# Decoder block on one core: the shift by the maxima in the mixing stage, half of it moved from TensorE to VectorE

## The reference, cut to what matters

```
logits = (x @ phi_w.T + phi_b)            # tokens x (64 experts x 32 slots)
C = softmax(logits, axis=2)               # over the 64 experts, for each token and slot
Y = einsum('tznp,npH->tzH', C, Y_tilde)   # mix 2048 slot outputs into each token
x = layernorm(x + Y)
```

## Time and profile before

| | us |
|---|---|
| median of 3 runs | 1799.91 (1797.38 to 1803.08) |
| the profiled execution's own time | 1800.99 |
| its span, first to last instruction | 1799.2 |
| PE busy in the span | 1625.1 (90%) |
| DVE busy | 1269.0 (71%) |
| POOL busy | 897.9 (50%) |
| ACT busy | 805.4 (45%) |
| first `mix_L` matmul starts at | 1215.82 |
| last `mix_res` starts at | 1796.54 |

### The profile page before, as it was taken

How to read it: one execution, slowest core, us unless ns; L and a number is a source line. 1 busy time by engine, 2 the same in 40 slices (tenths; PEclk the granted TensorE clock), 3 DMA queues, 4 the chain that set the end, 5 groups by cost and what they waited for, 6 DMA issues and landing times. The chain is left out here.

```text
span 1799.2 us, 43419 instructions
## 1 busy us (share of the span) xinstructions
PE 1625.1 (90%) x16382; PEld 1321.2 (73%) x16382; DVE 1269.0 (71%) x2438; ACT 805.4 (45%) x1354; POOL 897.9 (50%) x848
## 2 busy tenths in 40 slices
PE   6776698988988989699999999979999999999998
PEld 5665476766766767477777777758999999999997
DVE  5998366666655666688888888866666666766665
ACT  2444143333333334355665566544444444444443
POOL 3333222222222222299999999954555555555554
PEclk8787599889988889899999999999999999999999
DMA  4110100000000000300000000000000000000000
GB/s 136 30 30 7 30 7 7 7 6 7 7 6 7 7 6 4 95 1 0 0 0 0 0 0 0 0 1 4 7 10 7 10 7 10 7 10 8 8 10 9
DMA packets 20165, 22.79 MB, mean 13 GB/s; under 512 B 2013, under 2 KB 14366, under 8 KB 20002
## 3 DMA queue, kind: packets, MB, share of 16 engines
q1 hardware_dynamic: 18402, 15.95, 3.2%
q0 software_dynamic: 1088, 4.19, 0.8%
q10 hardware_dynamic: 512, 0.23, 0.0%
HBM read 16.18 MB, written 4.19 MB: 11 GB/s over the span
## 5 line engine op out<-in xcount | busy, mean ns | idle before, releaser
L1295 POOL TENSOR_TENSOR mix_c<-mix_e,mix_rinv 128x1024 f32<-128x1024 f32 x128 | 243.5, 1902 | 135.7 <-DVE mix_rinv L1281 133.2
L1261 DVE TENSOR_REDUCE mix_mx<-mix_L 128x16 fp32r<-128x1024 f32 x128 | 156.8, 1225 | 166.7 <-PE mix_L L1217 166.7
L1016 POOL TENSOR_TENSOR gather_d<-gather_e,gather_rinv 128x1024 f32<-128x1024 f32 x128 | 245.0, 1914 | 50.8 <-DVE gather_rinv L991 42.8
L1232 PEld LDWEIGHTS mix_Y<-kept_phi,mix_cT 128*128 128x128 f32 x2048 | 248.2, 192 | 10.5 <-ACT mix_cT L1248 3.7
L1232 PE MATMUL mix_Y<-kept_phi,mix_cT 128*128 128x128 f32 x2048 | 249.5, 275 | 2.9 <-ACT mix_cT L1248 2.9
L1248 ACT COPY mix_cT<-mix_T 128x1024 f32<-128x1024 f32 x128 | 130.1, 1016 | 210.8 <-PE mix_T L1239 210.8
L782 POOL TENSOR_TENSOR cross_veps<-cross_mv,kept_eps 128x1 f32<-128x1 f32 x64 | 12.2, 190 | 383.2 <-DVE cross_mv L729 383.2
L959 ACT ACTIVATE gather_e<-gather_L 128x1024 f32<-128x1024 f32 x128 | 131.3, 1025 | 155.4 <-PE gather_L L926 155.4
L981 DVE TENSOR_REDUCE gather_mx<-gather_L 128x32 fp32r<-128x1024 f32 x128 | 156.8, 1225 | 34.5 <-PE gather_L L907 28.7
L987 DVE TENSOR_REDUCE gather_rsum<-gather_e 128x32 f32<-128x1024 f32 x128 | 156.2, 1220 | 32.0 <-ACT gather_e L959 30.5
L1252 ACT ACTIVATE mix_e<-mix_L 128x1024 f32<-128x1024 f32 x128 | 131.1, 1024 | 105.2 <-PE mix_L L1222 105.2
(11 more groups left out here) (201 smaller groups left out, 3722.6 us busy)
## 6 DMA issues: line engine op xcount, KB each, us to landing
attn_xTg<-in_xT SPq DMA_DIRECT2D x16, 256.0 KB, 2.6
kept_xres<-in_x POOLq DMA_DIRECT2D x4, 1024.0 KB, 11.4
out<-mix_res SPq DMA_DIRECT2D x32, 128.0 KB, 1.8
cross_cg<-in_ctxT SPq DMA_DIRECT2D x32, 58.5 KB, 1.7
setup_wT<-in_w_qkvT SPq DMA_DIRECT2D x1, 192.0 KB
kept_consts<-in_consts SPq DMA_DIRECT2D x1, 68.0 KB
first_xq<-in_xq ACTq DMA_DIRECT2D x1, 64.0 KB, 2.7
setup_wproj<-in_w_proj SPq DMA_DIRECT2D x1, 64.0 KB
```

The lines of the kernel that those rows point to most:

```text
L1016: pool.tensor_tensor(dd[tu.par][ju][:].rearrange("p i (n s) -> p i n s", n=16), e[ju][:], rinv[ju][:].rearrange("p (i n) -> p i n", i=2).u ...
L1232: ins = pe.matmul(psY[t % 2][:, 0:128], cT[u % 2][:, c, :], w.yk[:, 8 * (u % 2) + c, :], start=(u % 2 == 0 and c == 0), stop=(u % 2 == 1 a ...
L1261: dve.tensor_reduce(mx[u % 2][:].rearrange("t (i p) -> t i p", i=2), psL[u % 2][:].rearrange("t i (p n) -> t i p n", p=8), X, ALU.max)\
L1295: pool.tensor_tensor(cc[u % 2][:], e[u % 2][:], rinv[u % 2][:].unsqueeze(2).to_broadcast([128, 16, EXPERTS]), ALU.mult)\
```

## The change

- DVE gets a new instruction in each unit, behind the maxima: it subtracts the maxima of slots 0 to 7 from bank 0 and writes the result to a new SBUF tile `mix_low` (128 x 512, two buffers). It waits for its own maxima (`mx_ready`) and for the exponential that last read the buffer, and signals `low_ready`.
- PE shifts only bank 1: one matmul of 512 columns in place of two. Before it overwrites a pair of banks it waits for `low_ready` of unit u-2 too.
- ACT takes the exponential in two halves of 512: bank 1 from PSUM once the shift is done, then `mix_low` from SBUF once `low_ready` has come. `e_ready` is signalled by the second.

```diff
--- before.py
+++ after.py
@@ -1165,6 +1165,7 @@
     with ExitStack() as ctx:
         st = Store(nc, ctx, "mix")
         mx = [st.sb(f"mx{i}", [128, 16], F32R) for i in range(2)]
+        low = [st.sb(f"low{i}", [128, 8, EXPERTS]) for i in range(2)]
         e = [st.sb(f"e{i}", [128, 16, EXPERTS]) for i in range(2)]
         sums = [st.sb(f"sums{i}", [128, 16]) for i in range(2)]
         rinv = [st.sb(f"rinv{i}", [128, 16]) for i in range(2)]
@@ -1180,8 +1181,8 @@
         psT = st.ps("T", [128, 8, 128])
         psY = [st.ps(f"Y{i}", [128, 512]) for i in range(2)]
 
-        (l_made, mx_ready, shifted, e_ready, sum_done, rinv_ready, c_ready, cT_made, cT_ready, cT_read) = (
-            st.sem(n) for n in ("l_made", "mx_ready", "shifted", "e_ready", "sum_done", "rinv_ready", "c_ready",
+        (l_made, mx_ready, low_ready, shifted, e_ready, sum_done, rinv_ready, c_ready, cT_made, cT_ready, cT_read) = (
+            st.sem(n) for n in ("l_made", "mx_ready", "low_ready", "shifted", "e_ready", "sum_done", "rinv_ready", "c_ready",
                                 "cT_made", "cT_ready", "cT_read"))
         y_done, st_done, mv_ready, ve_done, rstd_ready, res_ready = (
             st.sem(n) for n in ("y_done", "st_done", "mv_ready", "ve_done", "rstd_ready", "res_ready"))
@@ -1211,6 +1212,7 @@
                 for u in units(k, 0):
                     at = slice(u // 2 * 128, u // 2 * 128 + 128)
                     reach(pe, e_ready, u - 1)
+                    reach(pe, low_ready, u - 1)
                     for n, (xs, ws) in enumerate(((w.xh, w.w2h), (w.xl, w.w2h), (w.xh, w.w2l))):
                         for i in range(2):
                             c = (2 * (u % 2) + i) * 512
@@ -1218,11 +1220,9 @@
                     ins.then_inc(l_made, 1)
                 for u in units(k, 1):
                     pe.wait_ge(mx_ready, u + 1)
-                    for i in range(2):
-                        ins = pe.matmul(psL[u % 2][:, i, :], w.neg_ident[:],
-                                        mx[u % 2][:, 8 * i:8 * i + 8].unsqueeze(2).to_broadcast([128, 8, EXPERTS]),
-                                        start=False, stop=True, skip_group_check=True)
-                    ins.then_inc(shifted, 1)
+                    pe.matmul(psL[u % 2][:, 1, :], w.neg_ident[:],
+                              mx[u % 2][:, 8:16].unsqueeze(2).to_broadcast([128, 8, EXPERTS]),
+                              start=False, stop=True, skip_group_check=True).then_inc(shifted, 1)
                 for u in units(k, 3):
                     t = u // 2
                     pe.wait_ge(cT_ready, u + 1)
@@ -1249,8 +1249,9 @@
                 for u in units(k, 1):
                     act.wait_ge(shifted, u + 1)
                     reach(act, c_ready, u - 1)
-                    act.activation(e[u % 2][:].rearrange("t p n -> t (p n)"),
-                                   psL[u % 2][:].rearrange("t i x -> t (i x)"), ACT.Exp).then_inc(e_ready, 1)
+                    act.activation(e[u % 2][:, 8:16, :], psL[u % 2][:, 1, :].rearrange("t (p n) -> t p n", p=8), ACT.Exp)
+                    act.wait_ge(low_ready, u + 1)
+                    act.activation(e[u % 2][:, 0:8, :], low[u % 2][:], ACT.Exp).then_inc(e_ready, 1)
 
         @block.vector
         def _(dve):
@@ -1261,6 +1262,11 @@
                     dve.tensor_reduce(mx[u % 2][:].rearrange("t (i p) -> t i p", i=2),
                                       psL[u % 2][:].rearrange("t i (p n) -> t i p n", p=8), X, ALU.max)\
                         .then_inc(mx_ready, 1)
+                    dve.wait_ge(mx_ready, u + 1)
+                    reach(dve, e_ready, u - 1)
+                    dve.tensor_tensor(low[u % 2][:], psL[u % 2][:, 0, :].rearrange("t (p n) -> t p n", p=8),
+                                      mx[u % 2][:, 0:8].unsqueeze(2).to_broadcast([128, 8, EXPERTS]), ALU.subtract)\
+                        .then_inc(low_ready, 1)
                 for t in tiles(k, 5):
                     dve.wait_ge(cT_read, 2 * t + 2)
                     reach(dve, res_ready, t - 1)
```

## The result

| | before | changed |
|---|---|---|
| median of 14 runs, us | 1800.05 (1796.24 to 1804.45) | 1807.19 (1803.52 to 1813.45) |
| profiled execution's span | 1799.2 | 1807.5 |
| PE busy | 1625.1 | 1614.0 |
| DVE busy | 1269.0 | 1349.4 |

The changed kernel is slower: the ratio is 1.0039, with a 95% interval of 1.0028 to 1.0051. The forecast was 1805 us, with a range of 1796 to 1813.

A forecast was written before the change was run, and what follows sets the result against it. PE was taken as the bound before, then waiting for POOL's mix_c in a 9.00 us loop. Pace +4.1, beginning +0.2, end +0.5 gave +4.8 us on the median of 1799.91: about 1805 us, range 1796 to 1813.

The forecast's parts named there:

- The loop: Y slot's logits, via DVE's maxima to reciprocal and POOL's mix_c, to PE's transposition: 0.65 us to spare before the change.
- The push: DVE's queue: everything behind the maxima moves 0.72 us later in each slot, with the subtraction taken as 684 ns.
- The pace: Mixing stage: a pair of slots takes 9.00 us in place of 8.933; over 61 pairs +4.1 us.
- The beginning: Start of the stage: first mix_c 0.65 us later, slots 3 and 4 each 0.215 faster; together +0.2 us.
- the clock falls: Rival: idle PE is granted less than full clock; at 0.9 on the mean about +32 us; chance 0.03.
- the prediction's own sign of being wrong: Mixing stage: the forecast is wrong if, among other signs, the granted clock there is below 1.00.
- The end: Last mix_c of a y slot holds up the last but one transposition by some 0.5 us: +0.5.
- The other parity: Plain slot's chain: nothing late; mix_c ends 2.26 us into the next y slot and is read at 3.34.
- PE as the bound: Rival: PE stays the bound at 8.50 us a pair, time 1774 us; chance 0.08.
- fell behind `mix_c`: Rival, plain slot: DVE's mix_res starts after POOL's mix_c and waits it out; pair 9.5 us, 1835 us; chance 0.04.
- The subtraction was not dear: Rival on DVE: the subtraction takes 1180 ns, push 1.22, pair 9.50 us, time 1835 us; chance 0.05.
- the 0.3% line: Whole kernel: 0.3% (5.4 us) is what measurement can tell from no change; slower 0.45, same 0.45, faster 0.10.

The follow-up runs named there:

- only the removal: Changed kernel without the subtraction: bank 0 not shifted by anyone, PE shifts bank 1, one exponential over both banks; 1774.14 us.
- only the addition: Kernel before plus the subtraction behind the maxima, its result unread; PE still shifts both banks, ACT takes one exponential; 1807.27 us.
- only the halves: Kernel before with only the exponential split into two of 512 columns, both from PSUM; 1801.94 us.
- GpSimd's order: Changed kernel, DVE's list untouched; POOL does mix_c of a y slot's unit ahead of mix_veps and mix_rstd; 1777.49 us.
- the subtraction twice: Changed kernel with a second subtraction in front of the first, into a tile nothing reads; 1846.77 us.

## Why the prediction was right

The number alone proves little: the range of 1796 to 1813 us took in the time of the kernel before, so it would have held with no effect at all. What was foretold of the mechanism is the better test. The sum below is taken from the one profiled execution of each of the two kernels.

- **What bounds it.** PE bound the kernel before, and one matmul less is worth 26 us where nothing else is late: shown by the kernel with only the removal (27.5 foretold).
- **The loop.** That the subtraction lies on a way from the logits back to PE was shown by placing it elsewhere (1774.58 in place of 1807.19), and by taking 0.6 us out of the same way on another engine (1777.49). That PE's relief turns into waiting was shown by the kernel with only the addition: 1807.27 with the matmul, 1807.19 without it.
- **The push.** 0.72 was foretold. `mix_low` took 692 ns, not 684, and from the maxima to `mix_y` there are now 1.87 us in place of 1.14: 0.73.
- **The pace.** 9.00 was foretold. Between the logits of slot 5 and of slot 127 there lie 1786.57 - 1236.11 = 550.46 us, 9.024 a pair; before it was 8.933. So the pairs cost 61 x 0.091 = 5.5 us in place of 4.1. Of the missing 0.02, 0.01 is the dearer subtraction; the rest is within the rounding of the starts that were added.
- **The beginning.** This is the term that was mis-sized most: 0.2 foretold, 1.8 measured (from the first logits to those of slot 5 it took 19.89 us, before 18.06). The 0.65 us by which the first `mix_c` was to be late came as 0.64. But PE stood idle for 2.41 us in front of the first transposition, and soon after, from 1225.9 to 1229.4, the granted clock was 1.2 GHz. Slot 3, which lies in that stretch, took 5.80 us from its logits to the next, where slot 4 took 4.27. The sum had no term for these 1.5 us. The rival "the clock falls" came true at this one place, and with it the prediction's own sign of being wrong (a granted clock in the stage below 1.00) for 3.4 us of 591. In the steady pace, with PE idle for 0.5 us in 9, the granted clock stayed at 1.00.
- **The end.** 0.5 foretold; from the last logits to `mix_res` it took 18.25 in place of 17.73.
- **The sum.** 5.5 + 1.8 + 0.5, and 0.4 by which the stage began later in this execution: 8.2 of the 8.3 us between the two spans. Between the medians there are 7.1, where 4.8 were foretold.
- **The other parity.** In the plain slot's chain nothing was to be late: `mix_c` was to end 2.26 behind the y slot's logits and to be read at 3.34. It ended at 2.26 (1498.19 + 1.90 in the changed kernel, logits at 1497.83), and the load that reads it started at 3.35.
- **PE's busy share.** 94% was foretold, and the row of matmuls shows 97% (96.99 of 100 us). The gap is there, but recorded matmuls cover a part of it. By the loads the wait is 31.8 us, and 30 were foretold.
- **ACT.** It had cover, as foretold: 597 ns and 622 ns for the halves, and the kernel with only these shows no difference.
- **The rivals.** PE as the bound fell, by the 63 waits. `mix_res` stayed at 0.26 us in the median and 0.35 at most. It never fell behind `mix_c` in the changed kernel; in four of the others (only the removal, only the halves, GpSimd's order, the subtraction twice) it did once for some 1.9 us, as in the earlier trace rows, and in the last of them a second time for 0.78. The subtraction was not dear, also beside `mix_c`: it took 690 to 694 ns in all 128 cases, among them the one that starts at 1505.02 in the timeline above, while `mix_c` ran from 1504.05 to 1505.95. The prediction's sentence on `low` should not be read as if one input in SBUF were enough to be free: `mix_res` reads one tile from SBUF too, beside its two numbers a token, and was held up in the earlier trace rows.

The time lies above the 0.3% line by little (1807.19 against 1805.45 us, and the ratio's interval takes in the line), in the part that had 0.45 beside 0.45 for no change. That it fell on the upper side is owed in part to the clock at the beginning, which was not in the sum. The mechanism could not say on which side of the line it would fall, since 0.01 us a pair is 0.6 us.

## What to carry to other kernels

An engine that is busy for 69% of the time is not free for new work at every place of its list: follow the start times from the bound engine round and back to it, and compare the loop's length with the bound engine's own work. In a hand-ordered pipeline a new instruction belongs behind the steps for which others wait, as late as its own reader allows; here that was worth 33 us for the same instructions. And look at what the other engines on the loop do first: two tiny instructions ahead of a long one on GpSimd were worth 30 us here, in the changed kernel. In the kernel before, where `mix_c` came 0.65 us early, that order was not tried.

## What the runs showed of the hardware

The granted clock at the stage's beginning was not expected. These are the first transposition of the changed kernel, the logits behind it and the maxima that they released:

```profile
1225.14 1.25 PE L1239 MATMUL mix_T<-kept_consts,mix_c 128*128 128x128 f32 x8 [2.41 <-POOL mix_c L1301]
...
1226.04 1.20 PE L1219 MATMUL mix_L<-kept_w2h,kept_xh 128*128 128x512 f32 x2
...
1228.98 1.23 DVE L1262 TENSOR_REDUCE mix_mx<-mix_L 128x16 fp32r<-128x1024 f32 x1 [2.66 <-PE mix_L L1219]
```

The changed kernel by stretches of 1 us (PE's busy time is the first number behind the comma, the granted clock the third from the end):

```profile
1223.00:1224.00 1.00, 0.00 (x0) 0.00 (x0) 1.00 (x2) 0.88 (x2) 0.82 (x1) 1.00 0.00 0
...
1225.00:1226.00 1.00, 0.86 (x8) 0.86 (x9) 1.00 (x1) 0.00 (x0) 0.09 (x1) 0.97 0.00 0
1226.00:1227.00 1.00, 1.00 (x5) 0.85 (x3) 0.29 (x2) 0.58 (x1) 0.60 (x1) 0.50 0.00 0
...
1229.00:1230.00 1.00, 1.00 (x8) 0.91 (x8) 1.00 (x1) 0.59 (x2) 0.00 (x0) 0.82 0.00 0
1230.00:1231.00 1.00, 1.00 (x11) 1.00 (x11) 0.96 (x3) 0.53 (x2) 0.00 (x0) 1.00 0.00 0
```

PE stood idle for 2.41 us, with the full clock still granted; half of it, 1.2 GHz, was granted only when PE was at work again, from 1225.9 to 1229.4. The logits of unit 3 released the maxima after 2.94 us (1226.04 to 1228.98) in place of 1.66, and the whole slot took 1.5 us longer than the next. The same fall shows in the four other kernels in which the first transposition waited for 2.41, 2.94, 2.96 and 3.34 us, and in none of the four in which it waited for 1.43 to 1.69. The fall does not always wait for PE to be at work: with the subtraction twice the clock fell at 1225.0, and PE started again at 1225.56. The kernel with only the addition showed it earlier, behind two idle times of 0.68 and 1.11 us, so the length of a single wait does not decide it alone; what does stays open. Waits of 0.5 us in each 9, or of 1.1 us in each 9.6 with the subtraction twice, left the clock at 1.00.

A subtraction of 128x1024 with a PSUM and an SBUF input took 1189 ns on the mean (1160 to 1225), and 692 ns for 128x512. The exponential of 1024 columns took 1057 ns from SBUF and 1024 from PSUM; of 512, 622 and 597.
